# A slot for every expert: the late weight parts move to VectorE's first slots, two row blocks' residual moves off TensorE, and the last rows are stored in two transfers

## The reference

```python
x = x + jnp.tanh(g_xattn[0]) * ssm(ctx_1024, layernorm(x))       # 16 states, 256 channels, scan over 256 steps
xn = layernorm(x).reshape(1024, 256)
logits = xn @ gate_w                                             # 8 experts
top_logits, top_idx = jax.lax.top_k(logits, 2)
top_w = softmax(top_logits)                                      # cw: the weight of each token for each expert
for e in range(8):
    h = silu(xn @ w0[e]) * (xn @ w1[e])                          # 256 -> 512
    out = out + cw[:, e:e + 1] * (h @ wo[e])                     # 512 -> 256
x = x + jnp.tanh(g_ffn[0]) * out
```

## Time and profile before

| | us |
|---|---|
| median of 3 runs | 297.42 (296.88 to 297.59) |
| the profiled execution's own time | 296.67 |
| its span, first to last instruction | 294.8 |
| TensorE busy | 262.5 (89%), 1170 instructions |
| VectorE busy | 227.1 (77%), 397 instructions |
| ScalarE busy | 187.9 (64%) |
| POOL busy | 179.4 (61%) |
| mean granted TensorE clock | 0.980 |

### The profile page before, as it was taken

One profiled execution on the slowest core, in us unless ns is written; L12 is line 12 of the kernel. 1 busy time (PEld: TensorE's weight loads), 2 busy tenths in 40 slices (PEclk: granted clock), 3 DMA queues, 4 the chain that ended last, 5 costly groups with the idle time before them and its releaser, 6 DMA issues.

```text
span 294.8 us, 4705 instructions
## 1 busy us (share of the span) xinstructions
PE 262.5 (89%) x1170; PEld 176.4 (60%) x1171; DVE 227.1 (77%) x397; ACT 187.9 (64%) x348; POOL 179.4 (61%) x162
## 2 busy tenths in 40 slices
PE   7995597899789898887889989999999999999970
PEld 7432242334335354533467658989898989898960
DVE  2889989999999998999967877665665666565640
ACT  2895758775775657778497646565657575757540
POOL 6013278999999898999870231547464646465342
PEclk9999799999999999999988999999999999999996
DMA  7699400000000001000089420333333333333312
GB/s 239 215 390 387 152 2 0 1 0 0 0 1 2 1 0 71 0 2 1 0 280 333 176 68 19 44 65 46 63 42 65 43 64 50 57 53 53 39 21 32
DMA packets 16659, 22.70 MB, mean 77 GB/s; under 512 B 2554, under 2 KB 10274, under 8 KB 16642
## 3 DMA queue, kind: packets, MB, share of 16 engines
q1 hardware_dynamic: 11456, 16.41, 15.9%
q0 software_dynamic: 4416, 6.03, 13.0%
q10 hardware_dynamic: 770, 0.06, 0.2%
HBM read 17.38 MB, written 5.11 MB: 76 GB/s over the span
## 4 chain that ended last, share of the span: by engine, by line
PE 63%; DVE 15%; issue 11%; POOL 6%; ACT 3%; POOLq 1%; DVEq 0%; ACTq 0%
PE PZ L1091 11%; PE PU L1055 11%; PE PD L1055 11%; PE PY L860 8%; DVE states L1256 5%; POOL hC L414 5%; PE PY L1077 4%; DVE states L1262 3%; PE PZ L1046 2%; PE PZ L912 2%; PE PY L855 1%; PE PU L768 1%; PE PD L805 1%; DVE W_lo L1356 1%; PE PU L846 1%
## 5 line engine op out<-in xcount | busy, mean ns | idle before, releaser
L414 POOL TENSOR_TENSOR hC<-states,WO 128x512 f32<-128x512 f32 x63 | 79.9, 1280 | 15.4 <-PE PY L860 10.3
L1262 DVE TENSOR_TENSOR_SCAN states<-PD,states 128x512 f32<-128x512 f32 x64 | 77.6, 1213 | 1.1 <-ACT PD L625 0.9
L860 PE MATMUL PY<-hC,ident 128*128 128x512 f32 x128 | 67.7, 612 | 4.2 <-POOL hC L414 4.1
L452 POOL DMA_INDIRECT out<-lg,y_at x23 | 36.5, 1585 | 49.3 <-ACT lg L734 41.9
L625 ACT ACTIVATE PD<-WO,Aneg 128x510 f32<-128x510 f32 x64 | 43.9, 689 | 18.4 <-DVE states L1262 15.2
L1256 DVE TENSOR_TENSOR states<-PU,WO 128x512 f32<-128x512 f32 x64 | 42.9, 672 | 1.3 <-POOL hC L414 1.0
L438 POOL DMA_INDIRECT hC<-x_rows,x_at x23 | 26.7, 1160 | 25.5 <-DMA x_rows<-u 15.0
L718 ACT ACTIVATE hidT_hi<-PY 128x512 fp32r<-128x512 f32 x23 | 13.8, 600 | 37.8 <-PE PY L1077 35.7
L1491 DVE TENSOR_TENSOR dA<-PU,dA 128x512 f32<-128x512 f32 x23 | 15.9, 692 | 28.4 <-PE PU L1055 28.4
L1503 DVE TENSOR_TENSOR WO_lo<-WO,WO_hi 128x512 fp32r<-128x512 f32 x46 | 29.7, 688 | 9.4 <-issue 9.3
L860 PEld LDWEIGHTS PY<-hC,ident 128*128 128x128 f32 x128 | 22.5, 191 | 16.6 <-POOL hC L414 11.2
(11 more groups left out here) (253 smaller groups left out, 504.3 us busy)
## 6 DMA issues: line engine op xcount, KB each, us to landing
W<-in_L_ffn_w SPq DMA_DIRECT2D x16, 512.0 KB, 10.9
WO<-in_L_ffn_wo SPq DMA_DIRECT2D x8, 512.0 KB, 6.3
xs<-in_x SPq DMA_DIRECT2D x2, 512.0 KB, 5.4
out<-xs SPq DMA_DIRECT2D x2, 512.0 KB, 3.2
x_rows<-u SPq DMA_DIRECT2D x2, 512.0 KB, 4.8
early<-in_ctx SPq DMA_DIRECT2D x1, 512.0 KB, 4.1
hC<-x_rows,x_at POOLq DMA_INDIRECT x23
out<-lg,y_at POOLq DMA_INDIRECT x23, 3.8
```

The costliest lines, as they stand in the source:

```text
L414: pool.tensor_tensor(hC[:, n % 2, :], states[:, n % RING, :], C_rep[:, pair % C_RING, :], ALU.mult).then_inc(hc_done, 1)
L452: pool.indirect_dma_start(out=out, out_offset=bass.IndirectOffsetOnAxis(ap=y_at[:, s:s + 1], axis=0), in_=y_tile[s % 2], in_offset=None, c ...
L860: pe.matmul(PY[:, h, :], ident[:, :], hC[:, n % 2, :], start=False, stop=(m == DS - 1)).then_inc(y_done, 1)
L1262: dve.tensor_tensor_scan(states[:, n % RING, :], DEC[n % 2], states[:, n % RING, :], 0.0, ALU.mult, ALU.add).then_inc(scan_done, 1)
```

## The change

The 14 late lower parts (`LATE`) are all made by VectorE, two ahead of `hidden(0, 0)` and two in each of the slots 0 to 5. `GATE_LOW` and `UP_LOW` say for which slot TensorE waits for which count of them. That an expert's part is there in time rests on the order of the slots: `iota_k` is -1 for the first tile of an expert, so that each expert has at least one slot even without tokens, and slot s never belongs to an expert above s. TensorE loses its four `low_part` and gets spins (products whose result isn't used) in their place: `SPINS` = 4 before TABLE, 1 behind it, 2 around `x_turn(0)`. `add_x(1, 0)` is left out: `add_gz(1, 0)` writes its bank afresh and VectorE's `residual` adds x. ScalarE's `x2_out(2)` goes with it, and the counts of x2_ok change. Slots 0 and 1 are in another order: `gate(1)` stands ahead of `hid_turn(0)`, `x_turn(2)` ahead of it. TensorE's slots 1 to 7 and VectorE's 0 to 5 are written out and the loops start later. The second half's rows are stored in two transfers of 256 rows, each as soon as its blocks are there. No other instruction is changed.

```diff
-WARM = 1
-POOL_SPLITS = tuple(range(EARLY, EARLY + 4))
-PE_SPLITS = tuple(range(EARLY + 6, EARLY + 10))
-DVE_SPLITS = tuple(range(EARLY + 4, EARLY + 6)) + tuple(range(EARLY + 10, len(SPLITS)))
+LATE = tuple(range(EARLY, EARLY + 8)) + (28, 29, 26, 27, 30, 31)
+GATE_LOW, UP_LOW = {3: 2, 4: 4, 5: 6, 6: 8, 7: 12}, {6: 10, 7: 14}
+SPINS = (4, 1, 2)
...
+            def store_pair(b):
+                sp.wait_ge(xn_ok, 2 * b + 2)
+                sp.dma_start(x_rows[b * L:(b + 1) * L, :].rearrange("(p r) d -> p r d", r=2), xn[:, 2 * b:2 * b + 2, :]).then_inc(x_stored, 16)
...
-            store_rows(1)
+            store_pair(2)
+            store_pair(3)
...
+            pool.wait_ge(consts, 11)
+            pool.memset(iota_k[:, :, 0:1], -1.0).then_inc(consts, 1)
...
-            for i in POOL_SPLITS:
-                lower(i)
-
-            pool.wait_ge(x_stored, 16 * NQ)
+            pool.wait_ge(x_stored, 16 * (NQ + 1))
...
-            x2_out(2)
             x2_out(3)
...
-            for j in range(len(PE_SPLITS)):
-                act.wait_ge(W_lo_ps, j + 1)
-                act.activation(lo_part(PE_SPLITS[j]), SPLIT[j], ACT.Copy).then_inc(W_lo_act, 1)
...
                 for l in range(2):
                     for h in range(2):
-                        mm = pe.matmul(x2[:, l, h, :], z_cols[:, q * QBLK + 2 * r + h, l, :], scaled_id[:, :], start=False, stop=(l == 1 and h == 1))
+                        alone = q == 1 and r == 0
+                        mm = pe.matmul(x2[:, l, h, :], z_cols[:, q * QBLK + 2 * r + h, l, :], scaled_id[:, :],
+                                       start=alone, stop=(alone or (l == 1 and h == 1)))
...
+            def spin(times):
+                for _ in range(times):
+                    pe.matmul(PD[1][:, :], ident[:, :], W1_hi[:, 0, 0, :].bitcast(F32), start=True, stop=True)
...
             router(1, 1)
-            add_x(1, 0)
+            pe.wait_ge(base_kept, 2)
...
-            for j in range(3):
-                low_part(j)
-            for _ in range(WARM):
-                pe.matmul(TABLE, ident[:, :], W1_hi[:, 0, 0, :].bitcast(F32), start=True, stop=True)
+            spin(SPINS[0])
...
-            low_part(3)
+            spin(SPINS[1])
...
+                if isinstance(s, int) and s in GATE_LOW:
+                    pe.wait_ge(W_lo_dve, GATE_LOW[s])
...
+                if isinstance(s, int) and s in UP_LOW:
+                    pe.wait_ge(W_lo_dve, UP_LOW[s])
...
-            keep_busy(1)
+            spin(SPINS[2] // 2)
             x_turn(0, 0, 16)
-            keep_busy(1)
+            spin(SPINS[2] - SPINS[2] // 2)
             pe.wait_ge(slots_ok, 1)
             first = expert_of(0)
-            pe.wait_ge(W_lo_pool, EARLY + len(POOL_SPLITS))
-            pe.wait_ge(W_lo_act, len(PE_SPLITS))
-            pe.wait_ge(W_lo_dve, 2)
+            pe.wait_ge(W_lo_pool, EARLY)
+            pe.wait_ge(W_hi_ok, len(SPLITS))
             gate(0, 0, first)
             x_turn(1, 1, 16)
-            pe.wait_ge(W_lo_dve, len(DVE_SPLITS))
             up(0, 0, first)
-            step(0, 0, 32)
-            step(1, 1, 32)
-            with pe.Fori(0, (SLOTS - 5) // UNROLL) as t:
+            second = expert_of(1)
+            x_turn(2, 0, 32)
+            gate(1, 1, second)
+            hid_turn(0, 0)
+            up(1, 1, second)
+            down(0, 0)
+            for s in range(1, 2 + UNROLL):
+                step(s, s % 2, 16 * (s // 2 + 2))
+            with pe.Fori(1, (SLOTS - 5) // UNROLL) as t:
...
+            def residual():
+                dve.wait_ge(x2_ps, QB + 1)
+                rows = xs[:, QBLK:QBLK + 2, :].rearrange("p t d -> p (t d)")
+                dve.tensor_tensor(rows, PZ[0][:, :], rows, ALU.add).then_inc(x2_dve, 1)
...
             link(dve.tensor_tensor(gap[:, :], top[:, :, 1], top[:, :, 0], ALU.subtract))
+            residual()
             row_stats(1, 0)
             places()
...
-            lower(DVE_SPLITS[:2])
             dve.scalar_tensor_tensor(out=y_at[:, :], in0=TABLE[:, 0:COLS], scalar=-1.0, in1=spare[:, :],
                                      op0=ALU.add, op1=ALU.add).then_inc(y_at_ok, 1)
-            lower(DVE_SPLITS[2:])
...
             split_x(1, 1)
+            lower(LATE[:2])
             hidden(0, 0)
-            with dve.Fori(0, (SLOTS - 3) // 2) as t:
+            for s in range(6):
+                split_WO(s, s % 2)
+                split_hidT(s, s % 2)
+                split_x(s + 2, s % 2)
+                lower(LATE[2 * s + 2:2 * s + 4])
+                hidden(s + 1, (s + 1) % 2)
+            with dve.Fori(3, (SLOTS - 3) // 2) as t:
```

More of the change, by code:

```diff
@@ L238, in build @@
         TABLE = bank[3]
-        SPLIT = [bank[i] for i in (4, 0, 1, 7)]
         x_rows = nc.dram_tensor("x_rows", [TOK, DX], F32, kind="Internal").ap()
@@ L268, in build @@
         W_hi_ok, W_lo_pool, W_lo_dve, xT_split = map(sem, ("W_hi_ok", "W_lo_pool", "W_lo_dve", "xT_split"))
-        W_lo_ps, W_lo_act, last_hc, mask_sum, count_ps = map(sem, ("W_lo_ps", "W_lo_act", "last_hc", "mask_sum", "count_ps"))
+        x2_dve, last_hc, mask_sum, count_ps = map(sem, ("x2_dve", "last_hc", "mask_sum", "count_ps"))
         w_hi_ok, w_lo_ok = sem("w_hi_ok"), sem("w_lo_ok")
@@ L326, in store_rows @@
                              xn[:, q * QBLK:(q + 1) * QBLK, :].rearrange("p (b r) d -> p b r d", r=2)).then_inc(x_stored, 16)
+            def store_pair(b):
+                sp.wait_ge(xn_ok, 2 * b + 2)
+                sp.dma_start(x_rows[b * L:(b + 1) * L, :].rearrange("(p r) d -> p r d", r=2), xn[:, 2 * b:2 * b + 2, :]).then_inc(x_stored, 16)
             def store_x2(q):
-                sp.wait_ge(x2_ok, (q + 1) * QB)
+                sp.wait_ge(x2_ok, QB + q)
+                if q:
+                    sp.wait_ge(x2_dve, 1)
                 sp.dma_start(out[q * QT:(q + 1) * QT, :].rearrange("(b p r) d -> p b r d", p=P, r=2),
@@ L692, in _ @@
             act.activation(egap[:, :], gap[:, :], ACT.Exp).then_inc(egap_ok, 1)
-            for j in range(len(PE_SPLITS)):
-                act.wait_ge(W_lo_ps, j + 1)
-                act.activation(lo_part(PE_SPLITS[j]), SPLIT[j], ACT.Copy).then_inc(W_lo_act, 1)
             act.preload_act_table_set("silu_and_others")
             act.wait_ge(ld["wo"], 16 * E)
-            act.wait_ge(x_stored, 16 * NQ)
+            act.wait_ge(x_stored, 16 * (NQ + 1))
             act.wait_ge(stored, 16 * NQ)
@@ L1033, in _ @@
             mm.then_inc(w_at_ps, 1)
-            def keep_busy(times):
-                pe.wait_ge(W_lo_act, len(PE_SPLITS))
-                for _ in range(times):
-                    pe.matmul(PD[1][:, :], ident[:, :], W1_hi[:, 0, 0, :].bitcast(F32), start=True, stop=True)
             def x_turn(s, i, loaded):
@@ L1282, in row_stat @@
             def row_stat(i):
-                dve.wait_ge(x2_ok, i // 2 + 1)
+                if i // 2 == QB:
+                    dve.wait_ge(x2_dve, 1)
+                else:
+                    dve.wait_ge(x2_ok, i // 2 + 1 if i < QBLK else QB + 1)
                 dve.bn_stats(stats[:, 1, i, :], xs[:, i, :]).then_inc(stats2_ok, 1)
+            def residual():
+                dve.wait_ge(x2_ps, QB + 1)
+                rows = xs[:, QBLK:QBLK + 2, :].rearrange("p t d -> p (t d)")
+                dve.tensor_tensor(rows, PZ[0][:, :], rows, ALU.add).then_inc(x2_dve, 1)
             def row_stats(q, r):
@@ L1368, in places @@
                 dve.wait_ge(count_ps, 1)
-                dve.wait_ge(consts, 16)
+                dve.wait_ge(consts, 17)
                 count = COUNT[:, 0:E].rearrange("p (e o) -> p e o", o=1).to_broadcast((P, E, NBLK))
```

## The result

The changed kernel takes 299.09 us (median of 20 runs, 297.28 to 299.83), against 297.27 us for the kernel before, measured beside it (20 runs, 294.32 to 298.83). The ratio is 1.0057, 95% interval 1.0036 to 1.0078: slower by 0.6%, where 295.2 and faster had been forecast. It ended on the side of the fourth rival, 0.4 under its 299.5.

What follows compares the result with a forecast made beforehand. TensorE, then VectorE, was taken to bind the routing stage, with TensorE pacing the slots. A gain of 3.0 at hid_turn(1), less 0.7 stall and 0.1 handovers, is 2.2: median 297.42 becomes 295.2, range 294.1 to 297.1.

Steps and rivals of the forecast that it cites:

- fourth rival: Clock stays down from the w_at matmuls through slots 0 and 1: zero gain at 5.8 us, 299.5; chance 0.07.
- (a): Routing stage, TensorE: add_x(1, 0), 1.91 us, goes; the second add_gz ends at 157.1 instead of 158.0.
- (b): Routing stage, VectorE: residual fills a wait, so `over` starts at 157.67 in place of 158.47, 0.80 earlier.
- (c): TABLE on TensorE: low_parts no longer set its time; x_at comes at 164.95 in place of 166.48, 1.5 earlier.
- (d): Last rows' store, split: second pair lands 2.15 after issue; first gather starts 1.45 earlier, at 166.1.
- (f): Slots 0 and 1: gate(1) fills hid_turn(0)'s wait of 0.8; hid_turn(1) could start at 178.7 against 181.65, 3.0.
- (g): VectorE's 14 lower parts in the first slots: one stall before hid_turn(1) gives back 0.7 of the 3.0.
- (e): First gate product: starts at 170.5, runs through to 171.9 in place of 174.09, 2.2 earlier.
- first rival: TensorE's clock falls between 161 and 168; one spell of 3.3 leaves a gain of 1.25, 296.2; chance 0.22.

Runs made afterwards that it cites:

- e2: The changed kernel with SPINS = (6, 3, 2) in place of (4, 1, 2): 296.02 us, ratio 0.9961.
- e8: e2 with the residual back on TensorE and ScalarE (add_x(1, 0) and x2_out(2) back, no residual on VectorE): 296.88 us, ratio 0.9973.
- e9: e2 with the last 512 rows stored in one transfer as before: 295.92 us, ratio 0.9947.
- e13: The changed kernel with SPINS = (6, 3, 2), POOL's four lower parts back on POOL and the old order of slots 0 and 1: 296.04 us.
- e5: e1 with POOL's four lower parts back on POOL, VectorE making ten: 295.50 us, ratio 0.9943.
- e1: The changed kernel with SPINS = (7, 2, 2) in place of (4, 1, 2), as many large products as before: 296.00 us, ratio 0.9960.
- e6: The changed kernel without the two spins around x_turn(0), SPINS = (4, 1, 0): 297.90 us, ratio 1.0015.
- e4: The kernel before with only the residual moved: add_x(1, 0) off TensorE, residual on VectorE, x2_out(2) off ScalarE: 296.72 us, ratio 1.0014.
- e10: The changed kernel with two spins more ahead of TABLE only, SPINS = (6, 1, 2): 297.71 us, ratio 0.9993.
- e12: The changed kernel with SPINS = (6, 3, 1) and POOL's four lower parts back on POOL: 294.34 us, ratio 0.9897.
- e11: The changed kernel with two spins more behind TABLE only, SPINS = (4, 3, 2): 298.67 us, ratio 1.0032.

## Why the prediction was wrong

**The steps up to the first gather** were right, and e2 shows it better than the changed kernel, whose early router end and long first spell happened to cancel. (a) and (b): `over` at 157.66 for 157.67; undone in e8, it costs 0.86 for 0.80. (c): x_at at 164.88 for 164.95. (d): the gather at 165.97 in e2 and 166.11 in the changed kernel for 166.1; its inner step, a landing 2.15 after the issue, is met in e2 (a median of 2.1 for the pair) and not in the changed kernel (2.7), where the gather came on time all the same, and e9 shows no gain from the split with these spins. The prediction's estimates of 3.2 and 2.6 us from the Trainium skill, "DMA: Bandwidth & Descriptors", use a fit that the page gives for transfers issued by GpSimd, and these stores are SyncE's; the traces have 2.8 to 3.2 for 512 KB and 2.1 to 3.1 for 256 KB. (f): worth 0.64 in e13, for the 0.8 of waiting that it fills. (g): a stall on dA, one, before `hid_turn(1)`, 0.7 forecast and 0.72 in e2, where the turn of x starts at 178.94, takes 0.22, and `hid_turn(1)` follows at 179.88; without the first four parts on VectorE (e5 against e1) 0.5 is gained. With the clock held the whole way comes to a gain of 1.76 in e2, for 2.2.

**The step that failed is in (c)**: "With spin for low_part(3) nothing on the path is left out", and with it the whole of (e), which prices the w_at matmuls, the spins and the first product from rows at full clock: due from 170.5 to 171.9, that product ran from 174.24 to 176.51. The kernel before had 6 large products of low_part and one warming product ahead of TABLE, and 2 behind it; the change leaves 4 and 1. That TensorE's products in this stretch did a second job, to keep the clock at 2.4 GHz for what follows, was seen, but only as the first rival, with one spell of 3.3 us and a chance of 0.22. What the runs showed in its place is a spell of 10.3 us. Its length is what was mis-sized: the stretch behind the fall is thin as well, and the clock did not come back in it; in e6, with still less in it, it took 13.7. That the thin work is why it took so long fits these two traces and wasn't tested by itself. The rule of the rival, 3.0 less L/2 less 0.1, gives with L = 10.3 a loss of 2.25; the profile has 2.62, of which up to 0.5 is the longer first spell, to 158.9. The fourth rival named the place nearly as it came (from the w_at matmuls into slot 0, not through slot 1), and its 5.8 us for zero gain and its 299.5 fit what was measured; it got 0.07, and the prediction gives no reason for so little. The one spell that it had to go by was of 3.3 us. A trace in which TensorE is kept at work in this stretch can't show how long a fall lasts when it isn't.

**The Trainium skill**, "TensorE: Matmul & The Clock Gate", Part 1, says that the default is throttled and activity releases it. The trace agrees (e1 against the changed kernel, 1.00 against 0.50), and the sentence should have weighed more than the one spell. The products alone don't keep every spell away, though: e4 had one, of 3.4 us, with all of them in place.

**What stays open.** The changed kernel's 20 runs spread from 297.28 to 299.83, those of before from 293.50 to 298.95 in the widest group. Where the spells lay is known for the profiled executions alone, and they differ between executions of like kernels (the first spell began at 152.1 in the changed kernel and is missing in e4, e10 and e12); for the others there is only the mean clock. What makes the clock fall in one execution and hold in another, and whether the place or the count of the spins matters, is open. The tail, from `hid_turn(1)` to the end, is 113.15 before and 114.2 in the changed kernel, so about 1 us of the difference of the two spans, 3.2, comes from there. Some 0.9 of it lies in the last scatters (the last three start at 283.53 to 292.17, 8.64 us, against 281.16 to 288.94, 7.78). It doesn't seem to belong to the change: the tail is 113.1 to 114.4 in the experiments' traces, and 114.2 in e4, which has the old slots.

## What to carry to other kernels

A product on an engine that seems to wait anyway may be what keeps its clock up: before taking work out of a thin stretch of TensorE, count the large products in it, and put back spins of the same length; here that was worth 3.1 us. Price a fall of the clock by what stands behind it, not by the one spell that the trace happens to have: if that is thin too, the fall can last (10.3 us here). Read the clock of all executions, not only of the profiled one. And where a change has several parts, each worth 1 us or less, a loss of several us from one of them hides that others work.

## What the runs showed of the hardware that I had not expected

Half clock lasted, once it had come: 13.7 us in e6, with TensorE written down as busy for 13.04 of them, and 10.3 in the changed kernel with 9.39 busy (2.49, 3.40 and 3.50 in the windows shown). A full "busy" isn't much work, though: TABLE's sixteen 24-column matmuls are busy for 2.42 us in the changed kernel, where a product of 512 columns has 0.86. The stretch just ahead of the fall was busy for 3.38 of 3.40, so a full busy time did not keep the clock there.

The mean clock of each run told which kernels had the long spells (0.956 to 0.970 against 0.976 to 0.987), and in e11 which executions.

At half clock 16 small matmuls of 48 columns took 3.61 against 1.97 or 1.70: they double like the large ones.

VectorE's product of two operands in SBUF took 1.79 beside POOL's subtraction and 0.69 without it, in the same place of the kernel: 1.78 or 1.79 in the six traces in which POOL makes its parts there, 0.69 in the eight in which it doesn't.
